# A Fourier-convolution and attention kernel on one core: image sums on TensorE, one root for two joined norms, fewer steps for token statistics

## The reference, cut to what matters

```python
def _inorm(x, w, b):                       # one mean and variance for each image
    y = (x - mean(x, (-2, -1))) * rsqrt(var(x, (-2, -1)) + 1e-5)
    return y * w + b
...
a  = _inorm(p + xa, attn_w, attn_b)        # the first joined norm
an = _inorm(a, norm2_w, norm2_b)           # the second, straight on its result
m  = _fno_layer(an, m0cw, m0sw, inner_norm=True, act=True)
m  = _fno_layer(m, m1cw, m1sw, inner_norm=True, act=False)
out = _inorm(m, mon_w, mon_b) + a
...
t = t + attn(_ln_t(t), ...)                # _ln_t: mean and variance over each token's 128 numbers
t = t + ffn(_ln_t(t), ...)
```

## Time and profile before

| | |
|---|---|
| median of 3 runs | 1945.04 us (1941.62 to 1947.04) |
| the profiled execution | 1941.3 us, its span 1939.5 us |
| TensorE (PE) busy | 1658.2 us, 85% |
| VectorE busy | 1525.4 us, 79% |
| ScalarE busy | 1027.1 us, 53% |
| GpSimd busy | 554.2 us, 29% |
| granted TensorE clock, mean | 0.942 of 2.4 GHz |

### The profile page before, as it was taken

One profiled execution on the slowest core, in us unless ns is written; L12 is line 12 of the kernel. 1 busy time (PEld: TensorE's weight loads), 2 busy tenths in 40 slices (PEclk: granted clock), 3 DMA queues, 4 the chain that ended last, 5 costly groups with the idle time before them and its releaser, 6 DMA issues.

```text
span 1939.5 us, 30247 instructions
## 1 busy us (share of the span) xinstructions
PE 1658.2 (85%) x11144; PEld 1022.0 (53%) x11144; DVE 1525.4 (79%) x3025; ACT 1027.1 (53%) x1522; POOL 554.2 (29%) x635
## 2 busy tenths in 40 slices
PE   8774777899699989269899999999899999999684
PEld 8650222499689989234444454444444454444342
DVE  5876999737876769779897998878988788884873
ACT  4388000123446244357777766676666766667620
POOL 1342676300074007313581031001271003000533
PEclk9896999999799999679999999999999999999897
DMA  6560345000000014000020012000131011000892
GB/s 171 227 157 12 90 104 111 2 1 1 1 1 1 1 40 142 3 1 1 1 52 25 1 33 44 12 1 12 22 88 31 25 55 55 12 11 2 287 377 105
DMA packets 131855, 112.42 MB, mean 58 GB/s; under 512 B 40192, under 2 KB 109184, under 8 KB 131168
## 3 DMA queue, kind: packets, MB, share of 16 engines
q1 hardware_dynamic: 130176, 107.41, 19.6%
q0 software_dynamic: 1536, 3.08, 0.5%
HBM read 82.37 MB, written 21.88 MB: 54 GB/s over the span
## 4 chain that ended last, share of the span: by engine, by line
PE 60%; DVE 20%; ACT 9%; issue 7%; POOL 1%; DMA 1%; SPq 1%; POOLq 0%; DVEq 0%; ACTq 0%
PE PS L552 5%; PE PS L554 5%; PE PS L553 5%; PE PS L571 5%; PE PS L572 5%; PE PS L573 5%; DVE U L1209 4%; PE PS L1507 4%; PE PS L1516 4%; PE PS L534 4%; ACT V L1723 4%; PE PS L1434 3%; PE PS L1659 3%; ACT Z L812 2%; DVE MI L978 2%
## 5 line engine op out<-in xcount | busy, mean ns | idle before, releaser
L809 ACT ACTIVATE Z<-PS,MI 128x1024 f32<-128x1024 f32 (+2 forms) x288 | 300.0, 1042 | 257.2 <-PE PS L554 220.6
L998 DVE TENSOR_TENSOR DB<-Z 128x1024 f16<-128x1024 f32 (+2 forms) x288 | 332.6, 1155 | 95.7 <-ACT Z L812 52.8
L978 DVE TENSOR_REDUCE MI<-PS 128x1 f32<-128x512 f32 (+2 forms) x576 | 356.5, 639 | 38.0 <-PE PS L534 21.5
L812 ACT ACTIVATE Z<-PS,MI 128x1024 f16<-128x1024 f32 (+2 forms) x288 | 298.3, 1036 | 0.0
L737 POOL TENSOR_SCALAR Z<-U,Z 128x128 f32<-128x128 f32 x104 | 65.3, 639 | 364.4 <-PE PS L573 243.2
L1209 DVE TENSOR_TENSOR U<-A,PS 128x1408 f32<-128x1408 f32 x108 | 166.2, 1611 | 1.6 <-PE PS L1625 1.6
L720 POOL TENSOR_SCALAR U<-U,Z 128x128 f32<-128x128 f32 x128 | 71.9, 577 | 325.8 <-DVE MI L1030 325.8
L1221 POOL TENSOR_TENSOR U<-A,U 128x1408 f32<-128x1408 f32 x36 | 113.8, 3190 | 88.4 <-DVE MI L1985 33.4
L1631 PE MATMUL PS<-U 128*32 128x352 f32 x1152 | 110.9, 481 | 0.1
L571 PE MATMUL PS<-Z,A 128*128 128x512 f16 (+3 forms) x288 | 104.5, 363 | 5.6 <-ACT CST L820 5.6
L1410 POOL TENSOR_SCALAR U<-U,MI 128x128 f32<-128x128 f32 x128 | 56.1, 452 | 183.2 <-DVE V L2081 183.2
(11 more groups left out here) (445 smaller groups left out, 3664.8 us busy)
## 6 DMA issues: line engine op xcount, KB each, us to landing
V<-in_L_ffn_weight SPq DMA_DIRECT2D x16, 1024.0 KB, 11.3
U<-in_L_ffn_weight SPq DMA_DIRECT2D x14, 1024.0 KB, 15.6
A<-x_planes SPq DMA_DIRECT2D x24, 528.0 KB, 9.6
U<-in_x SPq DMA_DIRECT2D x16, 512.0 KB, 4.3
V<-in_x SPq DMA_DIRECT2D x4, 2048.0 KB, 13.9
Z<-in_x SPq DMA_DIRECT2D x16, 512.0 KB, 4.7
out<-U SPq DMA_DIRECT2D x16, 512.0 KB, 3.5
token_rows<-U SPq DMA_DIRECT2D x16, 512.0 KB, 3.7
```

The lines of the kernel that those rows point to most:

```text
L809: act.activation(EX32[u % 2][:, 0:w], s, ACT.Exp, scale=SCALE / (QUP * KUP), bias=pb).then_inc(sem("ex_ev"), 1)
L812: act.activation(EHI[u % 3][:, 0:w], s, ACT.Exp, scale=SCALE / (QUP * KUP), bias=pb).then_inc(sem("hi_ev"), 1)
L978: dve.tensor_reduce(bm[:, g % 2, t, k:k + 1], PS[:, 4 + chunk_no[c] % 2, 0:w], AX.X, ALU.max).then_inc(sem("ch_ev"), 1)
L998: dve.tensor_tensor(ELO[u % 3][:, 0:w], EX32[u % 2][:, 0:w], EHI[u % 3][:, 0:w], ALU.subtract).then_inc(sem("lo_ev"), 1)
```

## The change

1. `row_moments` is gone. For images, TensorE sums the numbers of `ST` as they are (`image_sums`): four matmuls of 128 columns, each reading one of ST's columns 1, 4, 2 and 5 in steps of six numbers, and two over the squares of the row means, which VectorE makes meanwhile in one instruction (`image_squares`). `image_moments` combines the sums in four steps.
2. The second norm's variance is written as `e * (attn_w^2 + EPS) + EPS^2`, so that its scale needs one root and one reciprocal of its own and nothing of the first norm's. It is asked for first. The first norm's scale and shift are made after the last `half_evac` and before `a_ready`, and GpSimd waits for `a_ready`.
3. `token_variance` takes six steps instead of eleven, from the difference and the sum of the two half means; the first two wait for nothing. `batch_norm` takes three instead of four.

```diff
+        joined_w, joined_eps = par[:, 10:11], par[:, 11:12]
...
-        root_args = [rc[:, 0:4], istat[:, 2:3], WS[:, 3, :], WS[:, 5, :], image_var, image_var, WS[:, 3, :]]
+        root_args = [rc[:, 0:4], istat[:, 2:3], WS[:, 5, :], WS[:, 3, :], image_var, image_var, WS[:, 3, :]]
...
             def token_variance(n):
-                row_moments(n)
-                m, e, v = WS[:, 0, n], WS[:, 1, n], WS[:, 6, n]
-                later(dve.tensor_tensor(v, m, m, ALU.mult))
-                later(dve.tensor_tensor(v, e, v, ALU.subtract))
+                s = ST[:, n, :].rearrange("p n k -> p k n")
+                d, m, e, v = WS[:, 2, n], WS[:, 0, n], WS[:, 1, n], WS[:, 6, n]
+                dve.tensor_tensor(d, s[:, 1], s[:, 4], ALU.subtract)
+                dve.tensor_tensor(m, s[:, 1], s[:, 4], ALU.add)
+                later(dve.tensor_tensor(e, s[:, 2], s[:, 5], ALU.add))
+                later(dve.scalar_tensor_tensor(v, d, 0.25, d, ALU.mult, ALU.mult))
+                later(dve.scalar_tensor_tensor(v, e, 1.0 / 128, v, ALU.mult, ALU.add))
                 dve.tensor_scalar(v, v, EPS, None, ALU.add).then_inc(sem("var_ready"), 1)
...
             def batch_norm(b):
-                token_norm(n, 8 + b)
-                later(dve.tensor_scalar(tka[:, n], tkr[:, n], KUP, None, ALU.mult))
-                dve.tensor_scalar(tkb[:, n], tkn[:, n], KUP, None, ALU.mult).then_inc(sem("norm_ready"), 1)
+                dve.wait_ge(sem("root_ready"), 8 + b)
+                later(dve.reciprocal(tkr[:, n], WS[:, 1, n]))
+                dve.tensor_scalar(tka[:, n], tkr[:, n], KUP, None, ALU.mult)
+                dve.scalar_tensor_tensor(tkb[:, n], WS[:, 0, n], -0.5 * KUP, tkr[:, n], ALU.mult, ALU.mult).then_inc(sem("norm_ready"), 1)
...
+            pool.wait_ge(sem("a_ready"), 2)
             for i in range(N):
                 ins = pool.tensor_scalar(U[:, i, :], U[:, i, :], WS[:, 4, i:i + 1], WS[:, 5, i:i + 1], ALU.mult, ALU.add)
...
+            def image_sums(bank, n):
+                pe.wait_ge(sem("mv_ready"), n)
+                s = ST[:].rearrange("p n k -> p k n")
+                for i, k in enumerate((1, 2)):
+                    for half in range(2):
+                        pe.matmul(PS[:, bank, 128 * i:128 * i + 128], ones, s[:, k + 3 * half, :], start=half == 0, stop=half == 1)
+                pe.wait_ge(sem("mv_ready"), n + 1)
+                for half in range(2):
+                    mm = pe.matmul(PS[:, bank, 256:384], ones, WS[:, half, :], start=half == 0, stop=half == 1)
+                mm.then_inc(sem("mv_mm"), 1)
...
-            pe.matmul(PS[:, 7, 0:256], ones, MV, start=True, stop=True).then_inc(sem("mv_mm"), 1)
+            image_sums(7, 1)
...
-            pe.matmul(PS[:, 0, 0:256], ones, MV, start=True, stop=True).then_inc(sem("mv_mm"), 1)
+            image_sums(0, 3)
...
+            def image_squares(n):
+                dve.wait_ge(sem("mv_ready"), n)
+                s = ST[:].rearrange("p n k -> p k n")
+                dve.tensor_tensor(WS[:, 0:2, :], s[:, 1:5:3, :], s[:, 1:5:3, :], ALU.mult).then_inc(sem("mv_ready"), 1)
+
+            def image_moments(sums, mu, t, e):
+                later(dve.tensor_scalar(mu, sums[:, 0:128], 0.5, None, ALU.mult))
+                later(dve.tensor_tensor(t, mu, mu, ALU.mult))
+                later(dve.scalar_tensor_tensor(e, sums[:, 256:384], 0.5, t, ALU.mult, ALU.subtract))
+                later(dve.scalar_tensor_tensor(e, sums[:, 128:256], 1.0 / 128, e, ALU.mult, ALU.add))
+
+            later(dve.tensor_tensor(joined_eps, PAR["attn_w"], PAR["attn_w"], ALU.mult))
+            later(dve.tensor_scalar(joined_eps, joined_eps, EPS, None, ALU.add))
+            later(dve.tensor_tensor(joined_w, PAR["norm2_w"], PAR["attn_w"], ALU.mult))
...
-            later(image_stats(U, NIM - 1))
-            row_moments()
-            dve.memset(lay[:, 0:1], 0.0).then_inc(sem("mv_ready"), 1)
+            image_stats(U, NIM - 1).then_inc(sem("mv_ready"), 1)
+            image_squares(1)
             dve.wait_ge(sem("mv_mm"), 1)
-            later(dve.tensor_copy(mu, PS[:, 7, 0:128]))
-            later(dve.tensor_tensor(v, mu, mu, ALU.mult))
-            later(dve.tensor_tensor(e2, PS[:, 7, 128:256], v, ALU.subtract))
+            image_moments(PS[:, 7, 0:384], mu, v, e2)
+            dve.tensor_scalar(v2, e2, joined_eps, EPS * EPS, ALU.mult, ALU.add).then_inc(sem("var_ready"), 1)
             dve.tensor_scalar(v, e2, EPS, None, ALU.add).then_inc(sem("var_ready"), 1)
             dve.wait_ge(sem("root_ready"), 3)
...
             half_evac(1, NIM - 1)
+            dve.wait_ge(sem("root_ready"), 4)
+            later(dve.reciprocal(r, v))
+            later(dve.tensor_scalar(r, r, PAR["attn_w"], None, ALU.mult))
+            later(dve.tensor_tensor(v2, mu, r, ALU.mult))
+            later(dve.tensor_scalar(v2, v2, -1.0, PAR["attn_b"], ALU.mult, ALU.add))
```

More of the change, by code:

```diff
@@ L916, in take_weights, with vector_l1 @@
             dve.tensor_copy(mask16, cst["mask"]).then_inc(sem("fold_ready"), 1)
-        def vector_l1(dve, st, image_stats, row_moments):
+        def vector_l1(dve, st, image_stats):
             later = st.later
             def token_variance(n):
-                row_moments(n)
-                m, e, v = WS[:, 0, n], WS[:, 1, n], WS[:, 6, n]
-                later(dve.tensor_tensor(v, m, m, ALU.mult))
-                later(dve.tensor_tensor(v, e, v, ALU.subtract))
+                s = ST[:, n, :].rearrange("p n k -> p k n")
[5 more added lines that the diff above has]
+                later(dve.scalar_tensor_tensor(v, e, 1.0 / 128, v, ALU.mult, ALU.add))
                 dve.tensor_scalar(v, v, EPS, None, ALU.add).then_inc(sem("var_ready"), 1)
@@ L933, in token_norm @@
                 later(dve.reciprocal(tkr[:, n], e))
[L934 removed]
+                later(dve.scalar_tensor_tensor(tkn[:, n], m, -0.5, tkr[:, n], ALU.mult, ALU.mult))
             def batch_norm(b):
                 n = slice(NT * b, NT * b + NT)
[L939 to L941 removed]
+                dve.wait_ge(sem("root_ready"), 8 + b)
+                later(dve.reciprocal(tkr[:, n], WS[:, 1, n]))
+                dve.tensor_scalar(tka[:, n], tkr[:, n], KUP, None, ALU.mult)
+                dve.scalar_tensor_tensor(tkb[:, n], WS[:, 0, n], -0.5 * KUP, tkr[:, n], ALU.mult, ALU.mult).then_inc(sem("norm_ready"), 1)
             token_variance(slice(0, NT))
@@ L1680, in _ @@
                 inverse(layer)
-            pe.wait_ge(sem("mv_ready"), 2)
-            pe.matmul(PS[:, 0, 0:256], ones, MV, start=True, stop=True).then_inc(sem("mv_mm"), 1)
+            image_sums(0, 3)
             tensor_l1(pe)
@@ L2025, in image_stats @@
                 return ins
[L2027 to L2037, removed]
+            def image_squares(n):
[10 more added lines that the diff above has]
+            later(dve.tensor_tensor(joined_w, PAR["norm2_w"], PAR["attn_w"], ALU.mult))
+            dve.wait_ge(sem("once_mm"), ONCE["fold"])
             dve.wait_ge(sem("once_mm"), ONCE["fold"])
@@ L2146, in _ @@
             dve.wait_ge(sem("i2_ev"), 3 * NIM)
-            later(image_stats(Vn, NIM - 1))
-            row_moments()
-            dve.memset(lay[:, 0:1], 0.0).then_inc(sem("mv_ready"), 1)
+            image_stats(Vn, NIM - 1).then_inc(sem("mv_ready"), 1)
+            image_squares(3)
             dve.wait_ge(sem("mv_mm"), 2)
-            later(dve.tensor_copy(mu, PS[:, 0, 0:128]))
-            later(dve.tensor_tensor(v, mu, mu, ALU.mult))
-            later(dve.tensor_tensor(e2, PS[:, 0, 128:256], v, ALU.subtract))
+            image_moments(PS[:, 0, 0:384], mu, v, e2)
             dve.tensor_scalar(v, e2, EPS, None, ALU.add).then_inc(sem("var_ready"), 1)
@@ L2158, in _ @@
             later(dve.tensor_scalar(v, v, PAR["mon_w"], None, ALU.mult))
-            later(dve.tensor_tensor(b2, mu, v, ALU.mult))
-            dve.tensor_scalar(b2, b2, -1.0, PAR["mon_b"], ALU.mult, ALU.add).then_inc(sem("fin_coef"), 1)
+            later(dve.scalar_tensor_tensor(b2, mu, -1.0, v, ALU.mult, ALU.mult))
+            dve.tensor_scalar(b2, b2, PAR["mon_b"], None, ALU.add).then_inc(sem("fin_coef"), 1)
             dve.wait_ge(sem("fin_coef"), 1)
@@ L2170, in _ @@
             later(ins)
-            vector_l1(dve, st, image_stats, row_moments)
+            vector_l1(dve, st, image_stats)
 _INS = ['x', 'L0_conv_norm1_w', 'L0_conv_norm1_b', 'L0_conv_Kcw', 'L0_conv_Ksw', 'L0_conv_Qcw', 'L0_conv_Qsw', 'L0_conv_Vcw',
```

20 lines of the change are left out of this document (4 added, 16 removed).

## The result

| | before | after |
|---|---|---|
| median | 1944.67 us (1941.62 to 1947.04, 4 runs) | 1927.29 us (1923.88 to 1928.51, 4 runs) |
| the profiled execution | 1941.3, span 1939.5 | 1928.5, span 1926.4 |
| VectorE busy | 1525.4 us | 1513.1 us |
| granted TensorE clock, mean | 0.942 | 0.944 |

The ratio is 0.9903, with an interval of 0.989 to 0.9916: 18.9 us faster by the ratio, 17.4 by the medians. The forecast was 11.7.

A forecast was written before the change was run, and what follows sets the result against it. It took TensorE as the engine to feed, with VectorE's time alone paid in full. Joined norms 2.4, last norm 0.9, batch 0 1.7 and attention with its end 6.7 made 11.7 us off 1945.0: 1933.3, range 1927 to 1940.

The forecast's parts named there:

- Joined norms, sums: Image sums at the joined norms: TensorE starts at once with twelve instructions, VectorE goes on earlier, 1.27 us saved.
- Joined norms, chain: From the sums to the first write of V: 3.95 us instead of 7.09, 3.14 saved.
- What was moved: First norm's reciprocal and three steps behind the last bank, uncovered: TensorE waits 1.97 us more there.
- a fall in the new hole: Rival, chance 0.15: the clock falls in the longer hole before L1446, costing 1.7 us; whole time 1935.0.
- Last norm: Last norm of layer 0: the sums save the same 1.27 us, the chain has one step more; 0.9 saved.
- Token statistics of batch 0: Batch 0's statistics before ScalarE's root and GpSimd: 1.36 us from six steps, 0.32 from batch_norm, 1.7 saved.
- Attention: Five token-statistics blocks inside the loop: 4.1 us saved at three batches, 1.4 at two finished-row places, 5.5 together.
- The stall of 1 us in batch 1's block: Inside the attention: a 1 us stall that may not come back, counted only toward the range's lower end, 1927.
- End of the loop: End of the attention loop: TensorE's wait of 1.19 us for VectorE goes, 1.2 us saved.
- the attention gives nothing back: Rival, chance 0.13: shorter VectorE blocks in the attention uncover other waits; 6.2 us saved remain, 1938.8.
- the strided sums are slow: Rival, chance 0.02: strided matmul reads at both image sums cost far more, 1.3 us each, kernel about 1951.
- the change doesn't do what it says: Rival, chance 0.02: joined root leaves a second round trip on the path, keeping 2.8 us of 3.14; 1936.

The follow-up runs named there:

- the second measurement: The changed kernel run again with no edit: 1926.27 us, ratio 0.9897 to the kernel before.
- coef_early: Changed kernel with the first norm's reciprocal and three steps put ahead of the first write of V: 1930.22 us, one execution.
- coef_late: Changed kernel with the first norm's reciprocal and three steps behind the a_ready memset, GpSimd waiting on its own semaphore: 1922.32 us, 0.9878.
- loop_old: Changed kernel with the eleven-step token statistics back at the five places inside the attention's loop only: 1938.01 us, 0.9963.
- pad_late: Changed kernel with six extra waited VectorE steps behind the increment of var_ready at the five places in the loop: 1935.79 us, 0.9952.

## Why the prediction was right and wrong

The sign was right, and so were the terms outside the attention's loop, to within 1 us each. The size was too small: 1933.3 against 1927.3, the lower end of the range; the second measurement, 1926.3, lies just below it. By the ratio, 18.9 us were saved where 11.7 stood. The term that failed is the attention's: 5.5 us for the five blocks, where the loop gave 9.5. Step by step, by the traces:

- **Joined norms, sums: held.** TensorE started 0.02 us after the squares, the hand-over came 3.1 us after the statistics; I had 2.99. The doubt about the strided read is settled near its lower bound: 0.228 us an instruction, where the bounds were 0.213 and 0.43, or 0.12 us more for the eight. The Trainium skill (SBUF — State Buffer, on 16-byte cachelines) has a penalty for each new line. The trace agrees that there is one, of 0.015 us an instruction at this clock, and not of another 0.213, as the estimate had it.
- **Joined norms, chain: held.** 3.93 for 3.95. V came 4.33 earlier after the statistics; the two terms make 4.41.
- **What was moved: held at its place, missed beside it.** The idle time before L1451 grew by 1.74 (forecast 1.97). But the stretch from V to there grew by 0.8 only. The rest came back with the clock, which I had left as it was: around these norms it was at its lower level for 20.5 us before (from 501.8) and is for 13.7 now (from 503.5), so that the transform's first banks ran at full speed sooner. The experiments bear it out: with the same 0.82 of idle time the stretch takes 35.1 us where the clock was low for 20.5 us (the kernel before), 34.63 with 17.1 (coef_early) and 34.13 with 13.7 (coef_late). Windows at about the same distance from the first matmul, first of before, then of after:

```profile
519.00:522.00 3.00, 3.00 (x16) 3.00 (x16) 1.88 (x6) 3.00 (x9) 0.00 (x0) 0.50 0.00 0
```

```profile
516.00:519.00 3.00, 3.00 (x24) 3.00 (x23) 2.04 (x7) 3.00 (x9) 0.00 (x0) 0.80 0.01 3
```

  Up to the second half the joined norms gave 3.5 us (46.54 before, 43.01 now), of which the next stretch takes 0.2 back (128.93, now 129.16): 3.3 instead of **2.4**. The rival of a fall in the new hole did not come true: the clock stood at 1.00 from 548 to 552.
- **Last norm: held**, 0.95 and 0.84 for 0.9.
- **Token statistics of batch 0: held**, 1.73 for 1.7. The unwaited steps cost 0.12 and 0.13, as the row of the pair said. The Trainium skill (VectorE: DVE Perf Modes, "The DRAIN you can't avoid") says that leaving out the semaphores saves nothing, by which they would have cost as much as the waited one, 0.24; the trace does not agree. The same section also says that a next instruction that isn't held starts earlier, and that is what the trace shows.
- **Attention: the term that failed.** I put 5.5 us on the five blocks; the loop gave 9.5, and against loop_old 12.6. The batches' holes shrank by 4.02 for the **4.1** forecast. The first fault is "I take half, 1.4 for the two": the rows' holes shrank by 1.72 and 1.39, all of it, 3.1. My reason was that ScalarE loads its table whatever VectorE does. It does so (1370.85 before, 1361.84 now, in both as soon as its own work is done), but pad_late shows that the holes follow VectorE's time. The second fault is that the clock's falls behind the batches' holes were put at nothing in the sum; they stood only in a rival and in the range, as something that "may" be avoided. In the pair two were avoided (at batches 1 and 3, worth 2.4 and 1.7) and one was added (at the first rows, 1.7), 2.4 net. Holes and clock make 7.1 + 2.4 = 9.5. At the rows alone the two faults met: the hole that shrank by 1.72 got a fall that cost as much, so that both rows together gave 1.6, near the forecast 1.4, by luck; the batches gave 8.1. The stall of 1 us in batch 1's block, on which the lower end leaned, did not go: L926 lasts 1.30 there, as L2032 lasted 1.14 before, beside an addition of GpSimd's (L702) in both.
- **End of the loop: held**, 1.25 for 1.2: TensorE's wait at L607 is gone, and from L522 to the third L607 it takes 6.31 us instead of 7.56. The stretch gave 2.2. The 0.9 beyond the 1.25 are not traced to the change; along the experts the distance between the two profiles goes up and down with their waits.

The sum by stretches that repeat: 3.3 + 0.95 + 1.7 + 9.5 + 2.2 = 17.7, where 11.7 stood. The medians' 17.4 agree with it, and it lies within the ratio's interval, 16.3 to 21.4 us. The profiled pair shows 13.1, since it has the longer start (1.5) and the held-up subtractions (3.2) against it; whoever had only these two profiles would have called the forecast nearly right, by accident.

The rival "the attention gives nothing back" fell by loop_old, "the strided sums are slow" by the rows above, and that the change doesn't do what it says by the order of the rows.

## What to carry to other kernels

A small step on an engine for which TensorE waits is worth its length and, where the hole is near 2 us or more, the clock behind it: price such a hole with a share of a fall (mostly 1.4 to 1.7 us here, at 18 of 25 long holes, at none of those of 1.1 us or less), and don't halve a saving for a second engine unless a row shows TensorE waiting for that one. Small steps that don't read each other need no wait between them and cost half (0.12 against 0.24 us). And before a stretch's difference between two profiles is laid to a change, take a second profile of each: stretches that the change did not rewrite moved by more than some of its parts.

## What the runs showed of the hardware

- While GpSimd's additions of 128x1024 run (2.3 us each), VectorE's copies, casts and subtractions of a scalar that read and write SBUF can last up to 2.4 us instead of 0.2 to 0.27, several in a row; a copy that reads PS (L913, 0.21) and `bn_stats` (0.27 to 0.29 each) beside such additions did not. The cause is read from the timelines (they end when an addition does), no run took the additions away. The stretches that hold them differ by 4.1 us (changed kernel) and 5.2 us (kernel before) between two profiles of identical code.
- Holes of TensorE of 1.98 to 3.63 us had a fall of the clock to 1.2 GHz about them in 18 of 25 cases, those of about 1.40 us in two of seven, those of 0.70 to 1.11 us in none of 21. But the first finished rows had one in seven of seven short kernels with a hole of 1.90 to 2.08, and none in the first profile before and in loop_old with 3.62 and 3.63; and the new hole of 2.56 us at 548 had none. So the length of a hole alone does not decide it; what does was not found.
- A moving matrix of 128 columns read in steps of six float32 numbers takes 0.228 us an instruction at the lower clock, a contiguous one 0.213. At the full clock it was not measured.
- A fall of 3.4 us of the clock cost 1.4 to 1.7 us in the attention at batches 2 and 3 and the second rows, 0.5 to 2.4 at batch 1.
